# The routing's one-hots built one choice at a time, with the comparison number taken per partition and the token's number multiplied in

## The reference, cut to what matters

```
logits = flat @ router_w
scores = softmax(logits)
_, topk_idx = top_k(logits + router_bias, 4)
topk_scores = take_along_axis(scores, topk_idx); topk_scores /= topk_scores.sum()
comb = zeros((n, 64)).at[arange(n)[:, None], topk_idx].set(topk_scores)
g = silu(einsum('nd,edf->nef', flat, wg)); u = einsum('nd,edf->nef', flat, wu)
routed = einsum('ne,nef,efd->nd', comb, g * u, wd)
sg = silu(einsum('nd,sdh->nsh', flat, swg)); su = einsum('nd,sdh->nsh', flat, swu)
shared = einsum('nsh,shd->nd', sg * su, swd)
out = routed + shared
```

## Time and profile before

| | |
|---|---|
| median of 3 runs | 561.92 us (556.06 to 562.53) |
| the profiled execution | 556.62 us, span 554.8 us |
| instructions | 9043 |
| TensorE (PE) busy | 432.3 us, 78% |
| VectorE (DVE) busy | 321.6 us, 58% |
| ScalarE (ACT) busy | 257.9 us, 46% |
| GpSimd (POOL) busy | 182.4 us, 33% |
| chain that ended last | PE 64%, DVE 20%, ACT 7%, issue 6%, DMA 1%, POOL 1% |
| mean granted TensorE clock | 0.85 of full |

### The profile page before, as it was taken

The page is one execution under the profiler, slowest core; times in us unless marked ns, Lnnn a source line. Parts: engine busy times, 40 slices in busy tenths (PEclk is TensorE's granted clock), DMA queues, the critical chain, the costliest instruction groups (busy, mean ns, idle before and its releaser), DMA issues.

```text
span 554.8 us, 9043 instructions
## 1 busy us (share of the span) xinstructions
PE 432.3 (78%) x2742; PEld 285.2 (51%) x2742; DVE 321.6 (58%) x1049; ACT 257.9 (46%) x543; POOL 182.4 (33%) x297
## 2 busy tenths in 40 slices
PE   1787676998878668476789695988986999999970
PEld 1443333344444345363334542534645999999860
DVE  5657677655343375925622714535598666666758
ACT  2322224344456414446552575333166777777404
POOL 6011001222123401312230332110006777778770
PEclk9998875555798779969889898689796999999995
DMA  7790020000000000000000030119943666656632
GB/s 235 251 349 27 1 57 2 0 2 1 1 0 2 1 0 19 1 1 1 1 1 0 1 116 0 40 33 390 374 151 82 191 192 190 192 188 184 185 103 95
DMA packets 37754, 50.72 MB, mean 91 GB/s; under 512 B 3664, under 2 KB 29264, under 8 KB 37712
## 3 DMA queue, kind: packets, MB, share of 16 engines
q1 hardware_dynamic: 33104, 37.60, 20.0%
q0 software_dynamic: 4608, 12.59, 8.6%
HBM read 31.30 MB, written 18.87 MB: 90 GB/s over the span
## 4 chain that ended last, share of the span: by engine, by line
PE 64%; DVE 20%; ACT 7%; issue 6%; DMA 1%; POOL 1%; SPq 0%; DVEq 0%; POOLq 0%; ACTq 0%
PE PSUM L785 11%; PE PSUM L1105 11%; PE PSUM L729 6%; PE PSUM L1092 5%; PE PSUM L799 4%; PE PSUM L757 3%; PE PSUM L735 3%; PE PSUM L1083 3%; PE PSUM L923 3%; PE PSUM L950 2%; DVE st L1407 2%; PE PSUM L942 2%; PE PSUM L722 2%; PE PSUM L858 2%; ACT PR L1173 2%
## 5 line engine op out<-in xcount | busy, mean ns | idle before, releaser
L1173 ACT ACTIVATE PR<-PSUM 128x1024 f32<-128x1024 f32 (+1 forms) x96 | 81.6, 880 | 61.9 <-PE PSUM L799 61.6
L652 POOL TENSOR_SCALAR_AFFINE_SELECT PR<-PR 128x256 f32<-128x256 f32 x128 | 51.2, 416 | 161.9 <-ACT PR L1173 160.8
L1502 DVE CUSTOM_DVE_ANT_0 XN<-PSUM,XN 128x128 f32<-128x128 f32 (+3 forms) x128 | 56.2, 488 | 37.5 <-PE PSUM L757 37.3
L1105 PEld LDWEIGHTS PSUM<-QP,XT 128*128 128x128 f32 x512 | 68.6, 195 | 3.4 <-ACT QP L1362 0.2
L1105 PE MATMUL PSUM<-QP,XT 128*128 128x128 f32 x512 | 69.0, 279 | 0.0
L785 PE MATMUL PSUM<-PR,VA 128*32 128x256 f32 (+3 forms) x512 | 60.8, 571 | 8.8 <-DVE XT L1552 8.8
L799 PE MATMUL PSUM<-QT,KTr 32*128 32x384 f32 (+7 forms) x256 | 45.3, 431 | 13.4 <-ACT PR L1173 10.8
L757 PE MATMUL PSUM<-KTr,QT 32*128 32x128 f32 (+3 forms) x128 | 39.3, 536 | 12.7 <-DVE mx L1502 12.3
L519 POOL TENSOR_TENSOR QP<-QK,QP 128x128 f32<-128x128 f32 (+1 forms) x16 | 9.8, 610 | 118.6 <-ACT KP L507 67.3
L799 PEld LDWEIGHTS PSUM<-QT,KTr 32*128 32x128 f32 (+1 forms) x256 | 24.2, 223 | 45.7 <-issue 26.1
L685 POOL DMA_INDIRECT QP<-tokens,tok_of x24 | 23.8, 990 | 58.6 <-DVE tok_of L1823 51.6
(11 more groups left out here) (260 smaller groups left out, 790.2 us busy)
## 6 DMA issues: line engine op xcount, KB each, us to landing
expert_outputs<-PR SPq DMA_DIRECT2D x1, 8192.0 KB, 26.5
arena<-in_wgu SPq DMA_DIRECT2D x4, 2048.0 KB, 15.8
expert_outputs<-QP SPq DMA_DIRECT2D x64, 128.0 KB
arena<-in_wd SPq DMA_DIRECT2D x2, 2048.0 KB, 18.1
wq_sb<-in_wqkv SPq DMA_DIRECT2D x2, 768.0 KB, 5.4
X<-in_x SPq DMA_DIRECT2D x2, 512.0 KB, 4.4
QP<-in_wsgu SPq DMA_DIRECT2D x1, 1024.0 KB, 5.5
tokens<-XN SPq DMA_DIRECT2D x2, 512.0 KB, 6.7
```

Of the source, the lines that this page charges most:

```text
L652: ins = pool.affine_select(diag, diag, [[0, 2], [1, P]], ALU.is_ge, 0.0, base=0, channel_multiplier=-1)
L1105: mm = pe.matmul(bank(2 + 2 * part + r % 2)[:, 0:P], WB[:, r, w0:w0 + P], XGT[:, r, kt * P:(kt + 1) * P], start=(kt == 0), stop=(kt == KT ...
L1173: did(sc.activation(PR[:, n % PSLOTS, 2 * half:2 * half + 2, 0:WIDTH[chunk]], PSUM[:, 2 * half:2 * half + 2, 0:WIDTH[chunk]], ACT.Exp, sca ...
L1502: did(dv.tensor_tensor_reduce(MSK[m % 2][:, 0:nk], o[:, 0:nk], MASKQ[:, S - nk:S], op0=ALU.add, op1=ALU.max, scale=1.0, scalar=NEG, accum_ ...
```

## The change

The one `tensor_tensor` for 8 choices becomes 8 `tensor_scalar` instructions, one a choice, which compare the f16 row of numbers with a number per partition (a pointer to one f32 column of `hi1` or `lo`). `HI1`'s has a second operation, a multiplication by `tokid` of the choice's token group, also read by pointer. `name_tokens` and its semaphore are gone; TensorE waits on `s_hi1` in its place. `hi1` and `lo` are f32 where `hi16` and `lo16` were f16, and one `settle()` between them is gone. Every instruction still adds to a semaphore, but `s_hi1` and `s_lo1` count groups as before.

```diff
@@ TensorE
                 if n % (2 * TOPK1) == 0:
                     pe.wait_ge(s_lo1, n // (2 * TOPK1) + 1)
-                    pe.wait_ge(s_named, n // TOPK1 + 2)
+                    pe.wait_ge(s_hi1, n // (2 * TOPK1) + 1)
@@ ScalarE
-            def name_tokens(g):
-
-                sc.wait_ge(s_hi1, g + 1)
-                for c in (2 * g, 2 * g + 1):
-                    ones = HI1[:, TOPK1 * c:TOPK1 * (c + 1), 0:NTILE]
-                    did(sc.activation(ones, ones, ACT.Copy, scale=tokid[:, c:c + 1]), s_named)
-
             for u in range(AT_ONCE, 2 * NSB):
                 shared_silu(u)
-                if u == 5:
-                    name_tokens(0)
-                if u == 6:
-                    name_tokens(1)
-                    name_tokens(2)
-            name_tokens(3)
             routed_exp(1)
@@ VectorE
-            with nc.allow_low_precision(reason="whole numbers up to 128"):
-                did(dv.scalar_tensor_tensor(out=lo16[:, :].rearrange("p (t k) -> p t k", k=TOPK1), in0=n4, scalar=-float(P), in1=slot4,
-                                            op0=ALU.mult, op1=ALU.add))
-                settle()
-                did(dv.tensor_scalar(hi16[:, :], hi[:, :], 1.0, None, ALU.add))
+            did(dv.scalar_tensor_tensor(out=lo[:, :].rearrange("p (t k) -> p t k", k=TOPK1), in0=n4, scalar=-float(P), in1=slot4,
+                                        op0=ALU.mult, op1=ALU.add))
+            did(dv.tensor_scalar(hi1[:, :], hi[:, :], 1.0, None, ALU.add))
...
             for g in range(NC // G1):
-                n = slice(g * G1, (g + 1) * G1)
-                half = slice(g * G1 % (NC // 2), g * G1 % (NC // 2) + G1)
-                did(dv.tensor_tensor(HI1[:, n, 0:NTILE], iota16[:, 0:NTILE].unsqueeze(1).broadcast_to([P, G1, NTILE]),
-                                     hi16[:, n].unsqueeze(2).broadcast_to([P, G1, NTILE]), ALU.is_equal), s_hi1)
+                for n in range(g * G1, (g + 1) * G1):
+                    did(dv.tensor_scalar(HI1[:, n, 0:NTILE], iota16[:, 0:NTILE], hi1[:, n:n + 1],
+                                         tokid[:, n // TOPK1:n // TOPK1 + 1], ALU.is_equal, ALU.mult),
+                        s_hi1 if n % G1 == G1 - 1 else None)
...
-                did(dv.tensor_tensor(LO1[g // 2][:, half, :], iota16[:, :].unsqueeze(1).broadcast_to([P, G1, P]),
-                                     lo16[:, n].unsqueeze(2).broadcast_to([P, G1, P]), ALU.is_equal), s_lo1)
+                for n in range(g * G1, (g + 1) * G1):
+                    did(dv.tensor_scalar(LO1[n // (NC // 2)][:, n % (NC // 2), :], iota16[:, :], lo[:, n:n + 1], None, ALU.is_equal),
+                        s_lo1 if n % G1 == G1 - 1 else None)
```

More of the change, by code:

```diff
@@ L308, in build @@
         hi = sb("hi", [P, NC])
-        hi16 = sb("hi16", [P, NC], f16)
-        lo16 = sb("lo16", [P, NC], f16)
+        hi1 = sb("hi1", [P, NC])
+        lo = sb("lo", [P, NC])
         wk = sb("wk", [P, NC])
@@ L405, in build @@
         s_lo1 = sem("s_lo1")
-        s_named = sem("s_named")
         s_tok = sem("s_tok")
```

## The result

In 22 runs of each the changed kernel has a median of 563.6 us and the kernel before 559.01 us. The ratio of their undisturbed runs is 1.0093, with a 95% interval of 1.0066 to 1.012: slower by 5.2 us (3.7 to 6.7), which is clear of noise and under 2%. The absolute numbers lie lower than the 561.92 us of the three runs shown before, which was a median of three.

What follows compares the result with a forecast made beforehand. VectorE's one-hots up to `tok_of` were taken to bound the path. Terms 12.8 + 0.45 - 7.42 - 0.1 + 0.1 = +5.8 us on the median gave 567.7 us (likeliest 567.5), own range 565 to 569, 8 in 10 within 560.5 to 572.

Steps and rivals of the forecast that it cites:

- The place: VectorE's one-hots up to `tok_of` set the path; GpSimd, gathers and tile loop move with it, microsecond for microsecond.
- What is removed: VectorE's eight `tensor_tensor`, 7.42 us; ScalarE's eight naming instructions, 0; the `settle()` between `lo` and `hi1`, 0.1 us.
- What is added: 64 `tensor_scalar` on VectorE, fixed parts plus elements, 12.8 us; `settle()` behind both tables in groups 0 and 1, 0.45 us.
- TensorE's last group: The last matmuls before `tok_of` may run at the lower clock, 0.87 us against 0.88 of cover; 0.1 us added.
- The sum: Whole kernel: 12.8 + 0.45 - 7.42 - 0.1 + 0.1 = +5.8 us, 1.0% slower.
- the forecast's own range: Whole time with elements from free to the f32 rate: 561.92 + 3.2 to + 6.8, 565 to 569 us; chance 0.62.
- the wide one: Whole time, range of 8 in 10, taking in D at the low end and A at the high: 560.5 to 572 us.
- A (the slow rate): The 64 new instructions' elements go at the f16 `tensor_tensor` rate, 1.04 ns each: +9.6 us, 571.5 us; chance 0.10.
- B (no overlap): Each of the 64 new instructions starts only when the one ahead has ended: +13 us, 575 us; chance 0.06.
- C (not slower): Same VectorE loop: a pair of instructions in 0.23 us, or naming held the path; 560 to 562 us; chance 0.05.
- D: Whole time: the sum is right but runs fall at the level of the lowest run shown, 556.06: 562 us; chance 0.17.

Runs made afterwards that it cites:

- the late ScalarE: Kernel before, with two ScalarE copies of the last group's one-hots ahead of their naming; stretch (start of `lo` to start of `tok_of`) 10.76 us against 10.48.
- the kernel with one pointer: Changed kernel, but HI1's instructions only compare and ScalarE names tokens as before; stretch (start of `lo` to start of `tok_of`) 13.30 us against 15.23.
- the kernel with the moved projection: Kernel with both tables turned (8 choices innermost), plus TensorE's last shared projection put behind the tables' matmuls; `lo` to `tok_of` 9.03 us, 1.0029 of the kernel before.

## Why the prediction was right, by its own steps

**The place.** VectorE set the length of the stretch and everything behind `tok_of` moved with it: 138.33 and 138.32 us from `tok_of` to the end. Right for this change. The reason given was too simple, though: that nobody waits for ScalarE's exponential before the gathered tile lands is wrong. VectorE's weights need it (416.82 against 416.85 us before), and they too set the start of the tile loop. It did no harm here because the change makes VectorE later and ScalarE earlier; where `tok_of` came sooner, the exponential held VectorE up by 1.42 us.

**What is removed.** The eight `tensor_tensor` were counted at 7.42 us, ScalarE's step at 0 and the `settle()` at 0.1. The first is borne out by the kernels that undo one half each (14.56 and 11.03 us). The second holds by the late ScalarE (0.3 us of room towards `tok_of`) and by the kernel with one pointer, where naming was back and the stretch as forecast. The third: L1761 to L1763 is 0.11 us after against 0.22 before.

**What is added.** The fixed parts, 0.19 and 0.13 us, read off single instructions and off four f32 ones, are right: 0.206 and 0.163 less 0.017 and 0.033 for elements give 0.19 and 0.13. The step that was off is "I take a value a little under it, 12.8 us": the 64 instructions take 32 x (0.206 + 0.163) = 11.8 us. I had placed f16 nearly at the f32 rate of 0.54 ns; the step grows by 0.26 ns an f16 element between 64 and 128 of them, and by another 0.26 with an f32 row, so f16 was at half of the f32 rate. The Trainium skill, page VectorE: DVE Perf Modes, section on the perf-mode tier table, had this rate, and the estimate by it, 11.9 us, is within 0.1 us of the measured 11.8. A row of one type does not price another type at the same rate.

**TensorE's last group.** Expected 0.82 us at the lower clock and 0.1 us late; it took 0.61 and was not late. Doubling the whole duration was wrong: from the higher clock to the lower one it grew by half, from 0.41 to 0.61.

**The sum.** Expected +5.8 us; the stretch shows +4.75 (11.8 + 0.47 - 7.42 - 0.11 = 4.74), the runs +5.2 (3.7 to 6.7). That the runs lie closer to +5.8 than the stretch does is inside their interval and no merit of the sum. The median of 563.6 us lies below the forecast's own range of 565 to 569 and inside the wide one of 560.5 to 572. The upper end of the own range, +6.8, is 0.2 above what its terms give (13.6 + 0.45 - 7.42 = 6.6). The time of 567.5 was 3.9 us too high: about 1 us by the element price, the rest because the median of three runs, 561.92, stands 2.9 us above the median of 22.

**The rivals.** A (the slow rate) needed steps of 0.257 and 0.263 us, where 0.206 and 0.163 were measured. B (no overlap): made true by a wait behind each instruction, it gives 23.24 us and not 15.23; the forecast had it at +13 us, the measured stretch is +12.8. The Trainium skill, page VectorE: DVE Perf Modes, section "The DRAIN you can't avoid", has the sentence on the empty pipeline that the prediction cites, and adds that a next operation which is not held starts earlier. The prediction left this half out; the steps of 0.206 us for a duration of 0.294 agree with it. C (not slower) is out, as 1.0066 is the interval's lower end. D was no mechanism but a level of the runs, 562 us, and it came half true: the median of the kernel before fell to 559.01, about midway between 556.06 and 561.92.

## What to carry to other kernels

On VectorE, count steps between starts and not durations, and split a step into a fixed part and elements. Here the fixed part is 0.13 us with one per-partition pointer and 0.19 with two pointers and a second operation, so cutting one `tensor_tensor` of 512 elements (0.61 us) into eight `tensor_scalar` of 64 makes it 2.7 times as long although each element goes four times as fast; at 128 elements it is nearly even (1.30 against 1.13). Work that is taken off another engine pays only if that engine was last, and a chain that three engines share (VectorE, ScalarE, TensorE) gives back only as much as the second slowest allows: each attempt to shorten VectorE's part here ran into TensorE or ScalarE. And follow a gain past the place where it is made: two kernels had `tok_of` 1.1 us sooner and the tile loop 0.4 us later. The one that brought the tile loop forward, by 0.7 us, had also moved work of TensorE behind the tables.

## What the runs showed of the hardware that was not expected

TensorE reads an f16 operand whose elements lie 16 bytes apart far more slowly: 8 matmuls of 64 columns took 1.08 to 1.14 us instead of 0.40 at the higher clock, and nearly the same whether both operands or the moving one alone had the step. Unlike the straight groups, these hardly feel the clock: 16 of them took 2.10 us where the clock was granted in full for their first part, and 2.12 us in the kernel with the moved projection, where 0.63 was granted over 412 to 414 us and 0.50 behind it. ScalarE took 1.42 us for two instructions of 128x256 f16 that read with the step of 16 bytes and wrote straight, against 0.90 in place and straight.

The granted clock can also fall while TensorE is busy. In the kernel with the moved projection it was 1.00 from 411 to 412 us, fell while the f16 groups with the step of 16 bytes ran behind a wait of 0.99 us, and stood at 0.50 over 414 to 416 us with TensorE busy all the time, through most of the projection; over 420 to 422 us it was 1.00 again.
